# First feed-forward of a four-layer model: all leaves for all tokens, against tokens sorted by leaf

## What is computed

```
for _ in range(DEPTH):
    score = jnp.einsum('nd,nd->n', xf, node_w[cur]) + node_b[cur]
    cur = 2 * cur + 1 + (score >= 0).astype(jnp.int32)
sel = jax.nn.one_hot(cur - N_NODES, N_LEAVES)
hidden = relu(jnp.einsum('nd,ldh->lnh', xf, w1) + b1[:, None, :]) * sel.T[:, :, None]   # h = 64
out = jnp.einsum('lnh,lho->no', hidden, w2) + sel @ b2                                  # o = 128
...
attn = softmax(jnp.einsum('bqd,bkd->bqk', q, k) * scale, axis=-1)     # q, k, v: the three trees
x = x + jnp.einsum('bqk,bkd->bqd', attn, v)
```

## Time and profile before

| | |
|---|---|
| median of 3 runs | 1263.0 us (1261.86 to 1264.03) |
| profiled execution | 1262.16 us, its span 1260.3 us |
| PE, DVE, ACT, POOL busy | 1066.9, 633.9, 518.1, 182.4 us |
| mean granted TensorE clock | 0.929 |

### The profile page before, as it was taken

The page is one execution under the profiler, slowest core; times in us unless marked ns, Lnnn a source line. Parts: engine busy times, 40 slices in busy tenths (PEclk is TensorE's granted clock), DMA queues, the critical chain, the costliest instruction groups (busy, mean ns, idle before and its releaser), DMA issues.

```text
span 1260.3 us, 12073 instructions
## 1 busy us (share of the span) xinstructions
PE 1066.9 (85%) x3752; PEld 460.1 (37%) x3752; DVE 633.9 (50%) x1123; ACT 518.1 (41%) x960; POOL 182.4 (14%) x160
## 2 busy tenths in 40 slices
PE   4898989898899999998847958677778999997677
PEld 2354545444222222222514633222224444442333
DVE  3213131332888778641513434799964555552443
ACT  4322222323367767675303435655552222226510
POOL 9000000000000000000173530366620000000000
PEclk9899999998799999998788979799997999999779
DMA  9600000020021212113013420000000000000001
GB/s 191 214 2 0 0 0 0 0 59 23 20 64 39 64 40 64 39 46 91 11 31 89 135 77 0 1 0 1 0 1 0 1 1 0 0 0 0 1 0 33
DMA packets 60307, 42.13 MB, mean 33 GB/s; under 512 B 17352, under 2 KB 57277, under 8 KB 60164
## 3 DMA queue, kind: packets, MB, share of 16 engines
q1 hardware_dynamic: 57956, 38.80, 11.3%
q0 software_dynamic: 2304, 2.76, 0.7%
HBM read 29.59 MB, written 13.67 MB: 34 GB/s over the span
## 4 chain that ended last, share of the span: by engine, by line
PE 61%; DVE 14%; issue 13%; ACT 8%; SPq 2%; DMA 1%; POOL 1%; DVEq 0%; ACTq 0%; POOLq 0%; another core or an unknown queue 0%
PE psum L566 59%; ACT sb_scr L1256 5%; DVE sb_scr L1736 3%; DVE sb_scr L1986 2%; DVE sb_scr L1995 2%; ACT psum L1256 1%; DVE sb_small L1697 1%; PE psum L1028 1%; SPq L347 1%; PE psum L1010 1%; DVE sb_x L1617 0%; DVE sb_h L1600 0%; ACT L1256 0%; DVE sb_scr L1638 0%; DVE sb_scr L1810 0%
## 5 line engine op out<-in xcount | busy, mean ns | idle before, releaser
L1256 ACT ACTIVATE sb_scr<-psum 128x512 f32<-128x512 f32 (+2 forms) x648 | 323.1, 537 | 491.9 <-PE psum L566 386.7
L566 PE MATMUL psum<-sb_h,sb_wide 128*128 (+1 forms) x448 | 226.4, 612 | 0.0
L1736 DVE TENSOR_REDUCE sb_scr<-psum 128x2 f32<-128x1024 f32 x128 | 154.3, 1223 | 43.7 <-PE psum L566 43.1
L566 PE MATMUL psum<-sb_scr,sb_wide 128*128 128x512 f32 x256 | 132.2, 598 | 6.1 <-DVE sb_scr L2057 6.1
L566 PEld LDWEIGHTS psum<-sb_h,sb_wide 128*128 128x128 f32 x448 | 86.0, 196 | 99.4 <-issue 99.0
L534 POOL DMA_INDIRECT expert_in<-sb_scr x32 | 31.2, 975 | 586.1 <-DVE sb_scr L1881 576.7
L1680 DVE TENSOR_SCALAR sb_scr<-psum,sb_b 128x512 f32<-128x512 f32 x48 | 36.0, 751 | 152.9 <-PE psum L566 152.9
L566 PE MATMUL psum<-sb_kstack,sb_qstack 96*128 96x512 bf16 x256 | 100.9, 406 | 6.4 <-DVE sb_scr L1736 6.0
L1256 ACT ACTIVATE sb_scr<-psum,sb_b 128x512 f32<-128x512 f32 x60 | 40.8, 687 | 159.2 <-PE psum L566 159.2
L566 PE MATMUL psum<-sb_qstack,sb_kstack 128*128 128x512 bf16 x256 | 99.1, 392 | 3.5 <-ACT sb_scr L1256 2.0
L566 PE MATMUL psum<-sb_wparts,sb_pick 96*128 96x512 bf16 (+1 forms) x192 | 66.4, 402 | 39.0 <-DVE sb_scr L1995 28.8
(11 more groups left out here) (222 smaller groups left out, 1299.8 us busy)
## 6 DMA issues: line engine op xcount, KB each, us to landing
sb_qstack<-q_bounce SPq DMA_DIRECT2D x48, 96.0 KB
sb_kstack<-k_bounce SPq DMA_DIRECT2D x144, 32.0 KB
expert_in<-sb_scr SPq DMA_DIRECT2D x4, 645.0 KB, 7.2
sb_scr<-expert_in SPq DMA_DIRECT2D x8, 322.5 KB
expert_out<-sb_scr SPq DMA_DIRECT2D x4, 512.0 KB, 5.9
sb_wide<-L_ffn_W SPq DMA_DIRECT2D x2, 1024.0 KB, 7.4
sb_scr<-expert_out SPq DMA_DIRECT2D x8, 256.0 KB, 4.7
q_bounce<-sb_scr SPq DMA_DIRECT2D x12, 128.0 KB, 2.4
```

What stands on the lines that cost most here:

```text
L566: return nc.tensor.matmul(out_, w, r, start=start, stop=stop, **kw)
L1256: return nc.scalar.activation(out_, in_, func, **kw)
L1736: v.reduce_max(headmax[:, g % 2, t:t + 2, j], banks, AX.X).then_inc(sem("maxed"), 1)
```

## The change

Each token now goes through its own leaf alone. The 2048 tokens of each tree are sorted by leaf: DVE computes for each token a slot in a table of 32 tiles of 128 rows, in which each tile belongs to one leaf (empty rows are zeros), and for each tile its leaf. POOL scatters the token rows to DRAM (`leaf_in`), 16 indirect DMAs for each tree. Then 24 chunks of four tiles pass: SP loads the token rows (256 KB) and three of the four leaves' weights, ACT the fourth and the store of the results (`leaf_out`); a leaf is 128 rows of 193 floats (w1, w2, b2, b1 side by side), chosen by a register that is read from `leaf_at`. PE turns the rows, multiplies by w1 (64 hidden units, two tiles in the upper and lower half of a bank), ACT clips, PE multiplies by w2. POOL gathers each tree's results back into token order, 16 indirect DMAs for each tree. The attention of all four batches then runs as one pipeline of 16 tiles, with the next block's layer norm and projections beside it. The packed weights are laid out by the host as an input. The clearing of `expert_in` moves behind the chunks. The separate parameter semaphores become one.

```diff
+TILES0 = 2 * NTOK // P
+CHUNK = 4
+NCHUNK = NTREE * TILES0 // CHUNK
+SLOTS0 = TILES0 * P
+WROW = LEAF_W + D + 1
+W_RING = 4 * CHUNK
...
+        for side, (rows_, one) in enumerate(((slice(0, LEAF_W), LEAF_W), (slice(LEAF_W, 2 * LEAF_W), 0))):
+            w[side, of, :, 0:LEAF_W] = inputs[f"L0_ffn_{name}_w1"]
+            w[side, of, rows_, LEAF_W:LEAF_W + D] = inputs[f"L0_ffn_{name}_w2"]
+            w[side, of, one, LEAF_W:LEAF_W + D] = inputs[f"L0_ffn_{name}_b2"]
+            w[side, of, rows_, WROW - 1] = inputs[f"L0_ffn_{name}_b1"]
...
+                leaf_table = leaf_in[f].rearrange("(n p r) d -> n p (r d)", n=4, p=P)
+                for n in range(4):
+                    sp.dma_start(leaf_table[n], blank[:, 0:8 * D]).then_inc(sem("leaves_cleared"), 16)
...
+            def load_leaves(c):
+                if c >= W_RING // CHUNK:
+                    sp.wait_ge(sem("tiles0_done"), c - W_RING // CHUNK + 1)
+                for g in range(c * CHUNK, c * CHUNK + CHUNK - 1):
+                    which = sp.value_load(leaf_at[0:1, g:g + 1], min_val=0, max_val=NTREE * LEAVES - 1)
+                    sp.dma_start(w_ring[:, g % W_RING, :], a["tree_rows"][g % 2][which]).then_inc(w0_loaded[c % len(w0_loaded)], 16)
+            def load_chunk(c):
+                f, n = divmod(c, NCHUNK // NTREE)
+                if n == 0:
+                    sp.wait_ge(qk_moved[f], ROWS0)
+                if c >= 4:
+                    sp.wait_ge(sem("rows_turned"), c - 3)
+                sp.dma_start(x_rows0[:, c % 4], leaf_rows_in[f][n]).then_inc(stacked[c % 4], 16)
+            sp.wait_ge(sem("leaves_known"), 1)
+            for c in range(W_RING // CHUNK):
+                load_leaves(c)
+            for c in range(3):
+                load_chunk(c)
+            for c in range(NCHUNK):
+                if c + 3 < NCHUNK:
+                    load_chunk(c + 3)
+                if c + W_RING // CHUNK < NCHUNK:
+                    load_leaves(c + W_RING // CHUNK)
+            sp.wait_ge(sem("blank_marked"), 1)
...
+            pool.wait_ge(sem("leaves_cleared"), 16 * 4 * NTREE)
+            pool.wait_ge(sem("h_rows_ready"), NB)
+            pool.wait_ge(sem("slots_known"), 1)
+            for f in range(NTREE):
+                for t in range(NT):
+                    nc.gpsimd.indirect_dma_start(
+                        out=leaf_in[f], out_offset=bass.IndirectOffsetOnAxis(ap=slot_at[:, t, f:f + 1], axis=0),
+                        in_=h_rows0[:, t, :], in_offset=None, bounds_check=SLOTS0 - 1, oob_is_err=False).then_inc(qk_moved[f], 16)
...
+            wait_for_tree(0)
+            for f in range(NTREE):
+                pool.wait_ge(qk_moved[f], ROWS0)
+            for t in range(NT):
+                gather0(0, t, qk_moved)
+            wait_for_tree(1)
+            for t in range(NT):
+                gather0(1, t, qk_moved)
+            wait_for_tree(2)
+            for t in range(NT):
+                gather0(2, t, v_moved)
...
-            def hidden_chunk(b, i):
-                f, c = divmod(i, HCH)
-                if i >= 3:
-                    pe.wait_ge(sem("hid_act" if (i - 3) % 2 == 0 else "hid_dve"), b * (n_hid // 2) + (i - 3) // 2 + 1)
-                mm(bank(i % 3), w1[f][:, c * P:(c + 1) * P], h[:, b, :], True, False)
-                mm(bank(i % 3), offpath[:, f, c, :], gates, False, True).then_inc(sem("hidden0"), 1)
...
+            picked0 = chosen0.rearrange("p (t f) n -> p t (f n)", t=NT)
+            for t in range(NT):
+                m = mm(psum[:, 6, 0:48], ones_b[:], picked0[:, t, :], t == 0, t == NT - 1, skip_group_check=True)
+            m.then_inc(sem("counted0"), 1)
...
+            def turn_rows(c):
+                pe.wait_ge(stacked[c % 4], 16 * (c // 4 + 1))
+                if c >= 2:
+                    pe.wait_ge(sem("xT_ready"), c - 1)
+                for j in range(CHUNK):
...
+                    m = nc.tensor.transpose(psum[:, c % 2, j * P:(j + 1) * P], x_rows0[:, c % 4, j, :], eye[:])
+                m.then_inc(sem("rows_turned"), 1)
...
+            def hidden_tiles(c):
+                pe.wait_ge(sem("xT_ready"), c + 1)
+                if c >= 2:
+                    pe.wait_ge(sem("hid_ready"), c - 1)
+                pe.wait_ge(w0_loaded[c % len(w0_loaded)], 16 * CHUNK * (c // len(w0_loaded) + 1))
+                for j in range(CHUNK):
+                    g = c * CHUNK + j
+                    m = mm(psum[leaf_side[j % 2], 2 + c % 2, j // 2 * P:(j // 2 + 1) * P], w_ring[:, g % W_RING, 0:LEAF_W],
+                           xT0[:, c % 2, j * P:(j + 1) * P], skip_group_check=True, tile_position=(0, j % 2 * LEAF_W))
+                m.then_inc(sem("hid0_done"), 1)
+            def out_tiles(c):
+                pe.wait_ge(sem("hid_ready"), c + 1)
+                if c >= 2:
+                    pe.wait_ge(sem("y_ready"), c - 1)
+                for j in range(CHUNK):
+                    g = c * CHUNK + j
+                    m = mm(psum[:, 4 + c % 2, j * D:(j + 1) * D], hidT0[j % 2][hid_depth[j % 2], c % 2, j // 2 * P:(j // 2 + 1) * P],
+                           w_ring[hid_depth[j % 2], g % W_RING, LEAF_W:LEAF_W + D], skip_group_check=True)
+                m.then_inc(sem("tiles0_done"), 1)
+            for c in range(NCHUNK + 2):
+                if c >= 2:
+                    out_tiles(c - 2)
+                if c < NCHUNK:
+                    turn_rows(c)
+                if 1 <= c <= NCHUNK:
...
+            def turn_qk(b):
+                pe.wait_ge(qk_moved[b], ROWS0 * (b < NTREE) + QK0)
+                if b == 0:
+                    pe.wait_ge(sem("y_ready"), NCHUNK)
                 else:
+                    pe.wait_ge(sem("qkv0_ready"), 2 * b)
+                for f in range(2):
                     for t in range(TT):
-                        m = mm(psum[:, 5, t * D:(t + 1) * D], hidden[:, c, t * P:(t + 1) * P], w2[f][:, c, :],
-                               c == 0 and t == 0, False, skip_group_check=True)
...
+            def values_out(b):
                 pe.wait_ge(sem("probsT0"), b * TT + TT)
-                pe.wait_ge(sem("qkv0_ready"), b * 3 + 3)
+                pe.wait_ge(v_moved[b], V0)
                 pe.wait_ge(x_ready, b + x_before(FFN0))
                 for k in range(TT):
-                    m = mm(bank(7), v0[:, k * D:(k + 1) * D], probsT0[:, k, :], k == 0, k == TT - 1)
...
+            beside = {(0, 0): lambda: turn_qk(1), (1, 0): lambda: turn_qk(2), (2, 0): lambda: turn_qk(3),
+                      (1, 2): lambda: center_one(ATTN1, 0, 5), (1, 3): lambda: variance_one(ATTN1, 0, 5),
+                      (2, 1): begin_q, (2, 2): lambda: project_k(0),
+                      (2, 3): lambda: center_one(ATTN1, 1, 5), (3, 0): lambda: variance_one(ATTN1, 1, 5),
+                      (3, 2): lambda: center_one(ATTN1, 2, 5), (3, 3): lambda: variance_one(ATTN1, 2, 5)}
...
+            turn_qk(0)
+            for n in range(NT):
+                b, t = divmod(n, TT)
+                if t == 0:
+                    pe.wait_ge(sem("qkv0_ready"), b * 2 + 2)
+                if n >= 2:
+                    pe.wait_ge(sem("exp0"), n - 1)
+                mm(bank(t % 2), qT0[b % 2][:, t * P:(t + 1) * P], kT0[b % 2]).then_inc(sem("scores0"), 1)
+                if (b, t) in beside:
+                    beside[b, t]()
+                if b >= 1 and t == 1:
+                    values_out(b - 1)
+                if n >= 1:
+                    attend(*divmod(n - 1, TT))
+            attend(NB - 1, TT - 1)
+            values_out(NB - 1)
...
+            def load_leaf(c):
+                if c >= W_RING // CHUNK:
+                    act.wait_ge(sem("tiles0_done"), c - W_RING // CHUNK + 1)
+                g = c * CHUNK + CHUNK - 1
+                which = act.value_load(leaf_at[0:1, g:g + 1], min_val=0, max_val=NTREE * LEAVES - 1)
...
+            for c in range(NCHUNK):
+                act.wait_ge(sem("hid0_done"), c + 1)
+                if c >= 2:
+                    act.wait_ge(sem("tiles0_done"), c - 1)
+                for j in range(CHUNK):
+                    g = c * CHUNK + j
+                    rows_, cols = leaf_side[j % 2], slice(j // 2 * P, (j // 2 + 1) * P)
+                    m = f(hidT0[j % 2][rows_, c % 2, cols], psum[rows_, 2 + c % 2, cols], ACT.Relu,
+                          bias=w_ring[rows_, g % W_RING, WROW - 1:WROW])
+                m.then_inc(sem("hid_ready"), 1)
+                if 1 <= c and c + W_RING // CHUNK - 1 < NCHUNK:
+                    load_leaf(c + W_RING // CHUNK - 1)
+                if c >= 2:
+                    store_chunk(c - 2)
+            for c in range(NCHUNK - 2, NCHUNK):
+                store_chunk(c)
...
+            st.then(lambda: v.reduce_sum(slot, place0, AX.X))
+            st.wait()
+            v.tensor_copy(slot_at[:].rearrange("p t f -> p (t f)"), slot).then_inc(sem("slots_known"), 1)
...
+            def begin_cut_q():
+                for r in range(4):
```

(32 more changed lines are left out.)

528 lines of the change are left out of this document (267 added, 261 removed).

## The result

The changed kernel takes 1307.1 us (median of 4, 1305.2 to 1312.2), the kernel before 1262.7 beside it: ratio 1.036, 95% interval 1.033 to 1.039. It is slower; I had said 1219, 1192 to 1252.

The account below looks back on a forecast made before the run. The first feed-forward, bound by TensorE's products over all 16 leaves, was to reach the projection of v at 271.7 instead of 315.9 us; 1263.0 - 44.2 = 1219 us, range 1192 to 1252.

Parts of the forecast that it names:

- the other 32 scatters lie beside the chunks: Scatter step: POOL's scatters for trees k and v, ending at 102 and 123 us, run beside the chunks.
- the gathers of q and k lie beside later chunks: Chunk step: POOL's gathers of q and k run beside later chunks; v's first four come by 208 us.
- My own sign of being wrong: Prediction wrong if chunks take over 5.3 us, or the next block's first scores wait for `k_bounce`.
- Rival C: SP's register read, three per chunk, uses up the gain at 1.4 us; at 1.65, 1279 us, slower; chance 0.14.
- the routing: DVE and TensorE before the scatters: steps sum to 18.0 us, slots known at 60.8 us.
- the scatters' rate: POOL's indirect scatters into the tables: 1.28 us each.
- a queue and transfers that fit under the chunk: Per chunk, SP's queue takes 3.8 us and transfers 4.2, both beneath the chunk's 4.6.
- the attention's period: Attention tiles: scores to maximum, shift, scaling and transposes add up to 3.2 us a tile; 15 are 48.
- bounce and next block waiting for nothing: After attention: q and k bounce starts near 251 us, first group in place by 264, so nothing waits.
- The chunk: TensorE's work on four tiles, with a 1.15 us wait for activations: 4.6 us at the lower clock, 2.9 at the higher.
- rival B: TensorE keeps the higher clock in the chunks; transfers bound at 4.2 us, attention starts warm: 1204 us; chance 0.18.
- The end of the attention: Last part of the attention pipeline, before the projection of v: 5.5 us at the higher clock.

Follow-up runs that it names:

- e10: Changed kernel with POOL's 96 indexed moves as plain DMAs in token order (rows meet wrong leaves), on a chip of the first kind: 1230.2 us.
- e6: Changed kernel unchanged, run on one chip of the first kind with two edited kernels: 1303.7 us.
- e5: Changed kernel run once more, unchanged, beside a kernel before of 1262.0 us: 1307.6 us, with the pauses.
- e17: Changed kernel unchanged, on a chip of the first kind beside a kernel before of 1260.7 us: 1306.6 us.
- e1: Changed kernel with weights loaded from fixed leaves, so no register reads on SP and ACT, on a chip of the second kind: 1229.2 us.
- e4: Changed kernel with weight loads after the first 16 cut to 16 of 128 rows, on a chip of the second kind: 1227.7 us.
- e7: Changed kernel without register reads (fixed leaves), on a chip of the first kind: 1292.1 and 1314.9 us in two executions.
- e14: Kernel of e10 with TensorE's output products of the chunk before moved behind turn and hidden products, first kind: 1244.9 us.
- e16: Kernel of e14 with SP asking for rows four chunks ahead and in front of the weights, second kind: 1206.0 us.
- e8: Changed kernel with only tree q's scatters on POOL, other scatters and all gathers replaced by memsets, first kind: 1236.6 us.
- e12: Kernel of e9 with TensorE's output products of the chunk before moved behind turn and hidden products, first kind: 1259.6 us.
- e9: Changed kernel with POOL's moves after tree q's scatters paced in small lots, first kind: 1253.9 us, ratio 0.992 to the kernel before.
- e3: Changed kernel with POOL's 96 indexed moves as plain DMAs in token order (rows meet wrong leaves), second kind: 1226.5 us.

## Why the prediction was wrong

Set beside my steps, in us from the span's start; e10 is nearly the same program without pauses:

| | forecast | e10 | changed kernel |
|---|---|---|---|
| first rows turned | 85.7 | 87.1 | 106.8 |
| last chunk copied out | 196.2 | 204.4 | 271.5 |
| projection of v | 271.7 | 283.9 | 361.3 |
| time of the execution | 1219 | 1230 | 1308 |

**The step that failed** is the sentence "the other 32 scatters lie beside the chunks", with "the gathers of q and k lie beside later chunks": I costed 80 of POOL's 96 moves at nothing. They cost 361.3 - 283.9 = 77.3 us: 19.7 up to the first rows (there the unbroken run of all 48 scatters slowed SP, and not tree q's 16 alone), 47.4 in the chunks, 10.2 in the attention. How this is shared out changes from one execution to the next: from the slots to the first rows the changed kernel took 44.0 us here, 28.8 in e6, 31.6 in e5 and 34.3 in e17, against 26.2 to 26.7 on the second kind. But the first results were copied out at 132.7, 130.8, 133.4 and 135.4 all the same, when POOL's 48 scatters were done (e1: 97.5). I had looked at POOL's own time, its transfers' bytes and who waits for the rows, and never asked whether a run of indirect DMAs takes something from engines that don't wait for it. The rows of before could not tell: under its 32 scatters SP issues nothing until they are done, and the other engines, which run out of work halfway (DVE at 644.8), are not slowed till then. My own sign of being wrong, chunks over 5.3 us, was there as well: 5.57 at the lower clock in e10, and up to 22.5 between two copies of turned rows in the changed kernel.

**Rival C had the sign, and the cause at most in part.** It put the loss on the register read, from 1.4 us on. One line's instructions, first SP's reads in the changed kernel:

```profile
L428 SPq TENSOR_LOAD <-sb_leaf_at x72: 1/270/1396, 66.8 to 253.4; - x72
```

then ACT's in the same kernel:

```profile
L1429 ACTq TENSOR_LOAD <-sb_leaf_at x24: 279/282/480, 66.8 to 251.4; - x24
```

and SP's in e4, without pauses:

```profile
L428 SPq TENSOR_LOAD <-sb_leaf_at x72: 262/268/538, 65.1 to 187.8; - x72
```

A read costs 0.27 us, half of the 0.56 that I took, and with all its company a load costs 1.11 (I had 1.14). What stretched SP to 3.2 us a load was the run beside it, together with the reads. A register move of the same line (ns min/median/max, first and last start) between 96 and 104 us, and between 134 and 138, when POOL had finished:

```profile
L429 SPq MOVE sb_scr<-tree_rows x2: 691/700/709, 95.5 to 103.9; - x2
...
L429 SPq MOVE sb_scr<-tree_rows x3: 29/29/29, 134.9 to 137.6; - x3
```

Without any read, e7 had no crawl but kept the pauses, and its time: so the reads matter for SP under the run, not for what was lost. The Trainium skill, page "DMA: Bandwidth & Descriptors" (section "Latency and other measured facts"), gives about 600 ns as the floor of such a load; these rows show medians of 268 to 282 ns, and the measurement decides.

**Right:** the routing (slots at 62.7 for 60.8; from 61.1 to 67.6 over all these kernels), the scatters' rate (1.28 us), a queue and transfers that fit under the chunk where nothing pauses, the attention's period (3.08 us for 3.2), bounce and next block waiting for nothing.

**Mis-sized terms, 12.2 us in e10.** The chunk: I had 4.6 us at the lower clock and it took 5.57, because an activation of 64x128 took 0.362 us, not 0.2 (my row was a 128x128 group of five that overlap, each 0.27 to 0.32 long), so that the hole behind the hidden products was 1.59 and not 1.15, and the output products 2.07 for 1.73. In part the clock was at the higher level (0.66 mean), which I had given to rival B: period 3.8 to 4.2 there. Net 117.3 us for 110.5, +6.8. The end of the attention took 7.5 us for 5.5, its tiles 67.1 for 65.3, its start +0.2. First rows +1.4: the slots came 3.2 late, and the rows 1.8 early, as e10's plain scatters are done sooner. By e14 to e16 the hole alone was not the bound: behind it stood SP's order, at once.

**Left open.** What in the chip the run holds up is not shown. The activations that ran kept their 0.362 us, so it is their release or their issue that came late; SP's small instructions, deep in the run, came every 0.70 us whatever they did. Loading of code is not what ended them: in the changed kernel no transfer of instructions started between 74.1 and 140.4 us, 176.7 and 217.8, or 219.2 and 255.5, where the three long pauses lie. Nor is a run alone enough, as the shared expert shows, and three maxima of the attention still came at 279.1, 282.4 and 285.5 us, beside v's gathers. The long pauses all lie where SP and ACT issue DMAs next to POOL's; no run takes these away under an indexed run, so that this is the condition is a guess. The Trainium skill, page "SBUF — State Buffer" (section "Who interferes with whom"), says that a DMA never contends with a compute engine, and has GpSimd's descriptor work as the one that starves; here the others wait while POOL keeps its 0.97 us, which that does not cover. Also open is why some chips have the pauses and others not, and whether it is the chip at all: one chip was seen twice (e6 to e8 and e12 to e14), both times of the first kind, neither of the second kind was. The changed kernel itself never ran on the second kind; e1 and e4, each close to it, took 1229.2 and 1227.7 us there and 1292 or more on the first, so I estimate some 1230 us there, faster than before and inside my range; it was not measured.

## What to carry to other kernels

A long run of GpSimd's indirect DMAs is not free because nobody waits for its rows. Beside queues that issue DMAs, count it as time in which SP may crawl and waits of ACT and DVE may end late, and cut it into lots of two or three with work between (that made e9 some 50 us faster than the changed kernel), or use plain DMAs where the order allows. When a wait is taken out of a loop over several engines, look at what queues behind the moved instruction in every other queue first: here TensorE's new order lost 15 us alone (e14 against e10), and won 20 with SP's (e16 against e3, both without pauses). And measure the control on the same chip as the experiment: four edits "cured" a fault that the chip under them did not show.

## What was not expected of the hardware

- On chips of the first kind a dense run of indirect DMAs (one each 1.25 to 1.28 us) stretched many of SP's register, move and DMA instructions from 0.02 to 0.34 us to about 0.70 us each, and ACT began up to 15.1 us after its products were done; 16 plain DMAs of the same bytes from POOL, issued in 8.7 us, did none of it. Where SP and ACT issued nothing, 20 us of such a run cost the other engines nothing.
- Chips differ: on two of the six chips of the experiments there was no such pause, and the kernel before itself took 1255.5 and 1256.0 us there against 1259.6 to 1264.4 on the other four.
- A register read from SBUF took 0.27 us on SP and 0.28 on ACT; a weight load at a read address 1.11 us of SP's queue in all.
